# Column weights kept in the PSUM bank of the distances instead of in an SBUF tile

## The reference

```python
ys = hh + dy + off[..., 0]           # 9 taps x 8 groups per pixel
xs = ww + dx + off[..., 1]
for oy in (0.0, 1.0):
    for ox in (0.0, 1.0):
        yy, xx = (y0 + oy, x0 + ox)
        wgt = (1.0 - jnp.abs(ys - yy)) * (1.0 - jnp.abs(xs - xx))
        ...
        out = out + jnp.where(valid, wgt, 0.0)[..., None] * g
```

## Time and profile before

| | |
|---|---|
| time, median of 2 executions | 1320.55 us (1318.87 to 1322.22) |
| span of the profiled execution | 1326.9 us |
| PE busy | 1078.8 us (81%) |
| DVE busy | 836.9 us (63%) |
| ACT busy | 583.9 us (44%) |
| POOL busy | 394.8 us (30%) |

### The profile page before, as it was taken

The page is one execution under the profiler, slowest core; times in us unless marked ns, Lnnn a source line. Parts: engine busy times, 40 slices in busy tenths (PEclk is TensorE's granted clock), DMA queues, the critical chain, the costliest instruction groups (busy, mean ns, idle before and its releaser), DMA issues.

```text
span 1326.9 us, 17127 instructions
## 1 busy us (share of the span) xinstructions
PE 1078.8 (81%) x5184; PEld 728.2 (55%) x5184; DVE 836.9 (63%) x1592; ACT 583.9 (44%) x1245; POOL 394.8 (30%) x340
## 2 busy tenths in 40 slices
PE   2574799689977899689987799679987799779857
PEld 2341575456645676456755576446755576556534
DVE  2786467955597456955588465975588456864232
ACT  1422543463435544454435634464435634454233
POOL 0274014610275004620157003640166003640000
PEclk9955699879997899869997999899997999789958
DMA  4122000000000000000000000000000000000000
GB/s 133 49 69 61 19 1 1 1 2 3 0 0 0 5 0 0 0 2 3 0 0 0 4 0 0 0 2 3 0 0 0 5 0 0 0 0 3 0 1 2
DMA packets 5326, 12.32 MB, mean 9 GB/s; under 512 B 1118, under 2 KB 2342, under 8 KB 5094
## 3 DMA queue, kind: packets, MB, share of 16 engines
q1 hardware_dynamic: 4782, 9.02, 2.6%
q10 hardware_dynamic: 494, 2.81, 0.7%
HBM read 11.30 MB, written 0.52 MB: 9 GB/s over the span
## 4 chain that ended last, share of the span: by engine, by line
PE 58%; DVE 17%; issue 11%; ACT 6%; POOL 6%; DMA 1%; DVEq 0%; POOLq 0%; SPq 0%; ACTq 0%
PE ps_y L546 18%; PE ps_h L521 6%; POOL sb_acc L1068 5%; PE ps_h L535 4%; PE ps_h L522 4%; PE ps_h L536 4%; PE ps_t L451 4%; DVE sb_prod L902 4%; PE ps_m L437 4%; PE ps_t L452 3%; PE ps_t L419 2%; PE ps_h L501 2%; DVE sb_hx L886 2%; ACT sb_xg L736 2%; PE ps_t L501 1%
## 5 line engine op out<-in xcount | busy, mean ns | idle before, releaser
L1068 POOL TENSOR_TENSOR sb_acc<-sb_acc,sb_prod 128x512 f32<-128x512 f32 x256 | 332.4, 1320 | 235.0 <-DVE sb_prod L902 234.1
L750 ACT ACTIVATE sb_hid<-ps_h 114x512 f32<-114x512 f32 (+1 forms) x256 | 150.2, 595 | 287.0 <-PE ps_h L522 286.6
L973 DVE TENSOR_TENSOR sb_hid<-ps_h,sb_hid 114x512 f32<-114x512 f32 (+1 forms) x256 | 172.1, 685 | 154.7 <-ACT sb_hid L750 150.6
L451 PE MATMUL ps_t<-sb_bdh,sb_hx 128*128 128x512 f32 x288 | 157.8, 548 | 70.2 <-DVE sb_prod L902 66.6
L546 PE MATMUL ps_y<-sb_hid,sb_w2s 114*64 114x256 f32 x768 | 205.8, 392 | 0.0
L902 DVE TENSOR_TENSOR sb_prod<-ps_t,sb_hy 128x512 f32<-128x512 f32 x256 | 170.7, 683 | 32.1 <-POOL sb_acc L1068 20.5
L451 PEld LDWEIGHTS ps_t<-sb_bdh,sb_hx 128*128 128x128 f32 x288 | 63.7, 221 | 136.5 <-DVE sb_prod L902 108.2
L736 ACT ACTIVATE sb_xg<-sb_xn,sb_gt 128x128 f32<-128x128 f32 x384 | 120.1, 390 | 25.0 <-DVE sb_gt L961 25.0
L452 PE MATMUL ps_t<-sb_bdl,sb_hx 128*128 128x512 f32 x288 | 129.9, 451 | 0.0
L546 PEld LDWEIGHTS ps_y<-sb_hid,sb_w2s 114*64 114x64 f32 x768 | 90.3, 136 | 64.7 <-issue 10.7
L521 PE MATMUL ps_h<-sb_xh,sb_w1s 128*114 128x256 f32 x384 | 117.3, 327 | 0.7
(11 more groups left out here) (169 smaller groups left out, 1756.6 us busy)
## 6 DMA issues: line engine op xcount, KB each, us to landing
sb_hid<-in_w1T SPq DMA_DIRECT2D x16, 171.0 KB, 3.1
sb_hid<-in_w3T SPq DMA_DIRECT2D x16, 171.0 KB, 3.0
sb_w2s<-in_w2T ACTq DMA_DIRECT2D x1, 1368.0 KB
sb_hid<-in_u1T SPq DMA_DIRECT2D x4, 256.0 KB, 3.9
sb_hid<-in_u2T SPq DMA_DIRECT2D x4, 256.0 KB, 3.7
sb_omx<-in_omxT ACTq DMA_DIRECT2D x1, 612.0 KB
sb_xT<-in_x SPq DMA_DIRECT2D x8, 64.0 KB, 2.1
sb_u3s<-in_u3T ACTq DMA_DIRECT2D x1, 512.0 KB
```

The source lines that it names most:

```text
L451: mm(tb[u % 2][:, :], w, bdh[:, h, :], start=True, stop=False)
L750: af(hid[0:ch, j % RING, :], h1[j % 2][0:ch, :], ACT.Silu).then_inc(s_act_s, 1)
L973: v.tensor_tensor(hid[0:ch, j % RING, :], h3[j % 2][0:ch, :], hid[0:ch, j % RING, :], ALU.mult).then_inc(s_dve_hid, 1)
L1068: g.tensor_tensor(acc[:, t, h, :], acc[:, t, h, :], prod[:, u % 2, :], ALU.add).then_inc(s_pool_acc, 1)
```

## The change

ACT's Abs writes back into the bank `mb` instead of into `hat`, its Relu works there too, and both DVE instructions of `column_weights` read `mb`. The tile `hat` goes. The bank is now in use until `column_weights(k)` is done, so PE's `columns(k+1)` waits for that (`s_dve_hx`) in place of the Abs, and ACT's wait for the DVE step of the tap before falls away.

```diff
-        hat = sb("hat", [P, NH * PIX])
...
                 if k == 0:
                     pe.wait_ge(s_act_ym, count(n + 1))
                 else:
-                    pe.wait_ge(s_act_abs, count(K * n + k))
+                    pe.wait_ge(s_dve_hx, count(K * n + k))
...
             def columns(n, k):
                 act.wait_ge(s_pe_xr, count(K * n + k + 1))
-                if k > 0 or not isinstance(n, int):
-                    act.wait_ge(s_dve_hx, count(K * n + k))
-                af(hat[:, :], mb[:, :], ACT.Abs).then_inc(s_act_abs, 1)
+                af(mb[:, :], mb[:, :], ACT.Abs).then_inc(s_act_abs, 1)
                 act.wait_ge(s_act_abs, count(K * n + k + 1))
-                af(hat[:, :], hat[:, :], ACT.Relu, scale=-1.0, bias=1.0).then_inc(s_act_hat, 1)
+                af(mb[:, :], mb[:, :], ACT.Relu, scale=-1.0, bias=1.0).then_inc(s_act_hat, 1)
...
                 o = V(hx[:, k % 3, :, :], [[1, NH * PIX]])
-                v.tensor_copy(o, hat[:, :]).then_inc(s_dve_hr, 1)
+                v.tensor_copy(o, mb[:, :]).then_inc(s_dve_hr, 1)
                 dve.wait_ge(s_dve_hr, count(K * n + k + 1))
-                v.scalar_tensor_tensor(out=o, in0=o, scalar=negb[:, 0:1], in1=hat[:, :], op0=ALU.mult,
+                v.scalar_tensor_tensor(out=o, in0=o, scalar=negb[:, 0:1], in1=mb[:, :], op0=ALU.mult,
                                        op1=ALU.add).then_inc(s_dve_hx, 1)
```

## The result

The changed kernel takes 1373.1 us (1369.41 to 1376.79), against 1320.55 us: a ratio of 1.039, with an interval of 1.033 to 1.046. Forecast were 1328 us and a range of 1303 to 1353. Its profiled execution has a span of 1374.3 us, 47.4 us more than the one of before.

A forecast was written before the change was run, and what follows sets the result against it. PE (58% of the chain of waits) and DVE (17%) were taken as what counts; +3.5 us for seven passes and +3.5 us for the first image, on 1320.55, gave 1328 us, 80% range 1303 to 1353.

The forecast's parts named there:

- What bounds the kernel: PE sets the pace among the expert pairs; from tap 3 on, whatever shortens DVE is mostly gained.
- DVE's pair, 1.40 us: In column_weights, copy at 0.65 us and scalar_tensor_tensor at 0.72 us, 1.40 us from start to end.
- ACT at no change: ACT's own two instructions were costed at no change; its wait for the DVE step moves to PE.
- The waits among the pairs, +1.3 and +1.0 us: PE's new waits at columns(1) and columns(2) among the expert pairs delay each pass by 1.3 and 1.0 us.
- columns(4), "PE stands for 2.2 us ... net 0": PE waits 2.2 us, making DVE's work 1.5 us late; tap 4's DVE step, 1.5 us shorter, makes that net 0.
- Taps 5 and 6, -1.5 and -0.5: Way to tap 5: tap 4's DVE step 1.5 us shorter; way to tap 6: 0.5 kept of 0.9 us.
- Tap 7, -1.1: Tap 6's pair is 1.15 us shorter; DVE has top and tap(5,1) to do while columns(7) waits: -1.1 us.
- Tap 8, +0.9: PE waits 0.9 us at columns(8), with gate_unit and tap(6,2) behind it where PE sets the pace: +0.9 us.
- The first image, +3.5: Later columns products delay taps 0 and 1 by 1.8 and about 1.5 us, 0 from tap 3: +3.5 us.
- The sum: +0.5 us a pass, +3.5 us for seven passes, with the first image's +3.5 us: total +7 us.
- the falling clock: Rival: the granted clock falls behind PE's new wait at columns(4), giving 1352 us, +2.4%; chance 0.18.
- The range: The 80% range of the whole kernel's time, 1303 to 1353 us, taking in most of the low-clock case.

The follow-up runs named there:

- fill_at_tap4: The changed kernel with the attention's queries product issued once more by PE ahead of columns(4) in the loop: 1367.53 us, ratio 1.034.
- fill_twice: The changed kernel with the queries product issued two more times by PE ahead of columns(4) in the loop: 1344.33 us, ratio 1.021.
- queries_first: The changed kernel with columns(4) placed behind the attention's queries product in PE's queue instead of ahead of it: 1343.51 us, ratio 1.018.
- late_from_tap4: The changed kernel with columns(k+2) behind tap(k,2) instead of ahead of it in PE's queue, for k = 2 and up: 1320.5 us, ratio 0.999.

## Why the prediction was wrong, step by step

- **What bounds the kernel:** right. PE among the pairs, DVE from tap 3 on.
- **DVE's pair, 1.40 us:** right; the copy's 0.68 us and the other's 0.75, with their starts 0.72 apart, are 1.47 us from start to end, at taps with and without POOL's adds. The row of a PSUM operand beside POOL's adds was the right one to price by. By the Trainium skill (SBUF — State Buffer, SBUF: two separate sides) it is DVE's ops with two SBUF inputs or in a two-port mode that GpSimd's ops lock out. The trace agrees: with a PSUM operand the two stay at 0.67 to 0.69 and 0.75 us. The runs show the durations, not the lock itself.
- **ACT at no change:** right, 0.584 and 0.582 us mean instead of 0.594 and 0.631.
- **The waits among the pairs, +1.3 and +1.0 us:** right, +1.40 and +1.00, and so was the statement that nothing absorbs them. PE's other waits were forecast as well as these: 1.31, 0.76, 2.12, 0.32, 1.25 and 1.24 us in the pass shown, for 1.3, 0.9, 2.2, 0.4, 1.4 and 0.9. This row is of the changed kernel, at columns(1):

```profile
363.22 1.13 PE L436 MATMUL ps_m<-sb_dwT,sb_omx 68*128 68x256 f32 x4 [1.31 <-DVE sb_hx L885]
```

- **columns(4), "PE stands for 2.2 us ... net 0":** this is the step that failed. The wait was right, 2.12 us, and so was what is queued behind it. Its price was taken as if the clock stayed at 1.00: +1.5 to tap 4 where +5.9 was measured. Of that the wait itself has 1.8, as in the high-clock passes of `fill_at_tap4`, and the fall the other 4.1, near the 4.3 that `fill_twice` measured by itself. That is 30 us over seven passes, most of the 45 between 1328 and 1373.1.
- **Taps 5 and 6, -1.5 and -0.5:** right (-1.37, -0.43).
- **Tap 7, -1.1:** wrong by the clock too, +0.22. In this pass a second fall lay over it; columns(7) took 2.07 us behind its wait of 1.25 us, and `tap(5,2)` stood behind it, for which DVE waited 1.86 us. Its lines:

```profile
412.67 2.07 PE L436 MATMUL ps_m<-sb_dwT,sb_omx 68*128 68x256 f32 x4 [1.25 <-DVE sb_hx L885]
...
415.72 0.69 DVE L899 TENSOR_TENSOR sb_prod<-ps_t,sb_hy 128x512 f32<-128x512 f32 x1 [1.86 <-PE ps_t L451]
```

The same was so in four passes of `fill_twice`, but in one of them columns(7) kept the high clock behind the same wait. The lines are columns(7) of two passes with a high clock at tap 4:

```profile
397.19 2.08 PE L440 MATMUL ps_m<-sb_dwT,sb_omx 68*128 68x256 f32 x4 [1.29 <-DVE sb_hx L889]
...
697.93 1.13 PE L440 MATMUL ps_m<-sb_dwT,sb_omx 68*128 68x256 f32 x4 [1.30 <-DVE sb_hx L889]
```

The way to tap 7 is 9.65 us in the first and 8.34 in the second. Against 9.43 before, 8.34 is the -1.1 of the forecast. So `top` and `tap(5,1)` do cover this wait; what was left out is again the fall.

- **Tap 8, +0.9:** mis-sized, +1.39 in this pass and +1.5 in the mean of the seven, at a mean clock of 0.51 to 0.64 on this way where the kernel before had 0.68 to 0.75.
- **The first image, +3.5:** mis-sized, +6.4 from its first copy to the next image's. The first copy itself came 0.9 later, which is not shown to be the edit's: over all the kernels it lies between 45.8 and 51.1 us. Taps 1 and 2 gave 3.35 of it, as forecast; taps 5, 6 and 8 gave 0.7 to 0.8 each, where I had taken 0 for shorter pairs against longer products.
- **The sum.** 7.2 up to the second image's first copy, 33.0 for six passes, 7.2 from the last image's first copy on: the 47.4 us of the spans. The passes of the kernel before varied from 147.0 to 153.6 us with its own falls of the clock, so a pass's difference is not the taps' difference alone: in the pass shown the taps lost 8.2 us and the rest of it won 4.7.
- **The rival that came true** was the falling clock, with 0.18. Its mechanism was right, the place too. Its time, 1352 us, was 21 below the result, since 3.5 us a pass were taken for a fall worth 4.3, and tap 7, tap 8 and the first image went wrong beside it. The argument against it, that short waits of PE lie about without a fall, compared shorter waits with one of 2.2, while the wait of that length in the pass, 2.33 us, had a fall behind it. The only longer one, 3.04 us at 400.46, lay within that fall, and even behind the 1.58 us at 411.21 the clock was 0.54 from 411.5 to 415.0. These rows should have decided; all are of the kernel before:

```profile
400.46 0.79 PE L451 MATMUL ps_t<-sb_bdh,sb_hx 128*128 128x512 f32 x1 [3.04 <-DVE sb_prod L902]
```

```profile
411.50:415.00 3.50, 3.50 (x16) 3.21 (x16) 2.73 (x5) 1.47 (x5) 2.47 (x2) 0.54 0.00 0
```

- **The range** ended at 1353: it ran to the rival's middle, not to the far side of it.

## What to carry to other kernels

When an edit moves a wait from an engine with slack to PE, price the clock as well as the wait: look for the waits of the same length that PE has already, and at the granted clock behind them. In this kernel one added wait of 2.1 us brought, in all seven passes, a fall worth 4.3 us, twice the wait. And before giving up an edit that shortens another engine's work at the price of such a wait, move independent work of PE's own queue ahead of it: here that turned +3.9% into -2.0%.

## What the runs showed of the hardware that was not expected

- The fall behind a wait is no fixed answer to that wait alone. With 0.51 us of it left it came in five passes of seven (`fill_at_tap4`) and in three of seven (`queries_first`), with none left in two of seven (`fill_twice`, `late_from_tap4`), in passes with identical instructions.
- The copy, which reads one SBUF tile only, also took longer beside POOL's adds: 0.41 to 0.43 us at taps 0 to 2 of every pass and up to 1.49 at the others from SBUF, and 0.673 to 0.692 in all 72 cases from PSUM.
- POOL gained also: its add took a mean of 1287 ns instead of 1320 (busy us, mean ns, idle before; the group of the changed kernel):

```profile
L1065 POOL TENSOR_TENSOR sb_acc<-sb_acc,sb_prod 128x512 f32<-128x512 f32 x256 | 325.2, 1287 | 296.4 <-DVE sb_prod L899 293.9
```
